# Cross attention: key products for two batches at once, value products for two batches in the other iterations

## What is computed

```python
def _L0_xattn_ref(query, key_value, Wq, bq, Wk, bk, Wv, bv, Wo, bo):
    H, D, scale = 16, 16, 16 ** (-0.5)
    q = (query @ Wq + bq).reshape(B, Nq, H, D).transpose(0, 2, 1, 3)
    k = (key_value @ Wk + bk).reshape(B, Nkv, H, D).transpose(0, 2, 1, 3)   # Nkv = 257, B = 64
    v = (key_value @ Wv + bv).reshape(B, Nkv, H, D).transpose(0, 2, 1, 3)
    attn = jnp.clip(jnp.einsum('bhqd,bhkd->bhqk', q, k) * scale, -CLAMP, CLAMP)
    attn = jax.nn.softmax(attn, axis=-1)
    x = jnp.einsum('bhqk,bhkd->bqhd', attn, v).reshape(B, Nq, Cq)
    return x @ Wo + bo
x = x + _L0_xattn_ref(_layernorm(x), ctx_768, ...)
```

## Time and profile before

| | |
|---|---|
| median of 3 runs | 593.39 us (592.71 to 594.58) |
| the profiled execution | 592.44 us |
| span of its trace, first to last instruction | 590.6 us |
| TensorE busy / weight loads busy | 579.2 us (98%) / 479.8 us (81%) |
| VectorE / ScalarE / POOL busy | 459.9 / 350.9 / 329.3 us |
| first `scores` of the loop | 18.34 us |
| last `scores` (iteration 63) | 328.11 us |
| granted TensorE clock, mean | 0.997 |

### The profile page before, as it was taken

The page is one execution under the profiler, slowest core; times in us unless marked ns, Lnnn a source line. Parts: engine busy times, 40 slices in busy tenths (PEclk is TensorE's granted clock), DMA queues, the critical chain, the costliest instruction groups (busy, mean ns, idle before and its releaser), DMA issues.

```text
span 590.6 us, 21921 instructions
## 1 busy us (share of the span) xinstructions
PE 579.2 (98%) x8431; PEld 479.8 (81%) x8431; DVE 459.9 (78%) x1064; ACT 350.9 (59%) x769; POOL 329.3 (56%) x481
## 2 busy tenths in 40 slices
PE   9999999999999999999999999999899999999997
PEld 4888878888788888788888788888478888887597
DVE  3688867888677887777777687698878888888496
ACT  4677867878777778677776444655433333333363
POOL 3456867878758788578887231011267666663000
PEclk9999999999999999999999999999899999999999
DMA  8625453676545745686430199535634334342895
GB/s 228 190 61 130 139 180 119 202 189 192 177 138 174 199 167 178 199 227 191 150 106 4 22 403 407 208 107 188 250 108 143 133 131 132 134 134 91 290 348 147
DMA packets 65399, 102.13 MB, mean 173 GB/s; under 512 B 15281, under 2 KB 41969, under 8 KB 64401
## 3 DMA queue, kind: packets, MB, share of 16 engines
q1 hardware_dynamic: 59200, 84.40, 45.2%
q0 software_dynamic: 4992, 15.34, 7.8%
q10 hardware_dynamic: 1104, 0.99, 0.6%
HBM read 69.43 MB, written 31.27 MB: 170 GB/s over the span
## 4 chain that ended last, share of the span: by engine, by line
PE 57%; POOL 20%; issue 14%; DVE 6%; DMA 1%; ACT 1%; POOLq 0%; SPq 0%; DVEq 0%
PE bank L2023 12%; PE scores L2023 6%; PE bank L1058 5%; PE bank L1065 5%; PE bank L1090 4%; POOL hA L732 4%; POOL lA L728 4%; PE bank L2051 4%; POOL hA L724 4%; PE scores L1106 3%; PE scores L1079 3%; PE scores L1242 2%; POOL Mb L765 2%; POOL tm L756 2%; PE bank L1017 2%
## 5 line engine op out<-in xcount | busy, mean ns | idle before, releaser
L864 DVE TENSOR_SCALAR Pm<-scores 128x514 f32<-128x514 f32 x128 | 88.1, 689 | 52.2 <-PE scores L1079 52.0
L980 ACT ACTIVATE Pm<-Pm,nm 128x257 f32<-128x257 f32 x256 | 115.7, 505 | 2.5 <-DVE nm L869 2.5
L869 DVE TENSOR_REDUCE nm<-Pm 128x2 f32<-128x514 f32 x128 | 87.5, 684 | 2.2
L975 ACT ACTIVATE PT<-bank 128x512 f32<-128x512 f32 x64 | 38.3, 598 | 74.1 <-PE bank L1090 74.1
L1058 PE MATMUL bank<-hA,wH 128*128 128x258 f32 x256 | 75.2, 305 | 0.1
L1090 PE MATMUL bank<-cst,Pm 128*128 128x128 f32 x512 | 70.0, 279 | 0.0
L1058 PE MATMUL bank<-hA,wL 128*128 128x258 f32 x256 | 69.3, 281 | 0.0
L1065 PE MATMUL bank<-wH,hA 128*128 128x256 f32 x256 | 68.9, 281 | 0.0
L1065 PE MATMUL bank<-wL,hA 128*128 128x256 f32 x256 | 68.8, 280 | 0.0
L2023 PE MATMUL bank<-W,xh 128*128 x208 | 66.6, 401 | 0.6 <-ACT xh L1943 0.6
L765 POOL TENSOR_TENSOR Mb<-Os,rc 128x64 f32<-128x64 f32 x64 | 21.7, 339 | 73.6 <-DVE rc L889 73.2
(11 more groups left out here) (299 smaller groups left out, 1428.7 us busy)
## 6 DMA issues: line engine op xcount, KB each, us to landing
w_d<-whl SPq DMA_DIRECT2D x64, 256.0 KB, 3.2
W<-w_d SPq DMA_DIRECT2D x6, 2048.0 KB, 17.7
wst<-in_W1T SPq DMA_DIRECT2D x32, 256.0 KB, 3.7
cg<-g_d SPq DMA_DIRECT2D x16, 512.0 KB, 5.8
cx<-in_ctxT SPq DMA_DIRECT2D x31, 258.0 KB, 3.0
cx<-in_ctxT SPq DMA_DIRECT2D x62, 129.0 KB, 3.6
bb<-in_b SPq DMA_DIRECT2D x8, 512.0 KB, 6.0
W<-w_d SPq DMA_DIRECT2D x5, 512.0 KB, 5.2
```

What stands on the lines that cost most here:

```text
L864: v.tensor_scalar(Pm[:, i % 2, 2 * p:2 * p + 2, :], S4[:, 2 * p:2 * p + 2, 0:NK], -CLAMP, CLAMP, ALU.max, ALU.min).then_inc(s_cl, 1)
L869: v.tensor_reduce(nm[:, i % 2, 2 * p:2 * p + 2], Pm[:, i % 2, 2 * p:2 * p + 2, :], AX.X, ALU.max, negate=True).then_inc(s_nm, 1)
L975: a.activation(PT[:, i % 2, 0, :, :].rearrange("p a b -> p (a b)"), held("p", i, 0)[:, :], ACT.Copy).then_inc(s_pte[0], 1)
L980: a.activation(Pm[:, i % 2, g, :], Pm[:, i % 2, g, :], ACT.Exp, bias=nm[:, i % 2, g:g + 1]).then_inc(s_ex, 1)
```

## The change

Keys of a pair of batches (2p, 2p+1) now come from one set of 10 products of 512 columns, 256 from each batch. They are made in the even iterations i = 2p-2. The odd iterations make the values of two batches, 20 products of 256 columns. At the edges the loop makes single batches of values: in -1 and 0, and in 61 and 62. The 257th key of all 64 batches is projected once ahead of the loop from `c256`, 4 short products into the bank of `vx`, and copied to `kE` by VectorE with the bias. From there ScalarE writes it for each pair into the last columns of `kT` (`last_keys`). `kT` holds two pairs instead of two batches. The splits on POOL change places: low parts in odd iterations, high parts in even ones, and they run one iteration earlier. `pace` is moved with them, and `wst0` gets another address.

```diff
@@ uses
+        def key_pair(i):
+            if i == -1:
+                return 0
+            return i // 2 + 1 if i % 2 == 0 and i + 2 < T else None
+        def value_batches(i):
+            if i in (-1, 0, T - 2):
+                return (i + 1,)
+            if i == T - 3:
+                return (i + 1,)
+            return (i + 1, i + 2) if i % 2 and i + 2 < T else ()
-        uses = [...] + [(("x",), s_vxe, 2)] + [...]
+        uses = [...] + [(("x",), s_vxe, 4)] + [...]
@@ POOL, loop
-                    j, n = (i + 3) // 2 if i % 2 else (i + 2) // 2, 0 if i % 2 else 2
+                    j, n = ((i + 3) // 2, 2) if i % 2 else ((i + 4) // 2, 0)
@@ VectorE, ahead of the loop
                 qevac(0)
+                for m in range(2):
+                    v.tensor_scalar(kE[:, m, :], held("x")[:, C + T * m:C + T * m + T], bcol[:, 2 + m:3 + m], None, ALU.add
+                                    ).then_inc(s_vxe, 1)
@@ ScalarE
+                def last_keys(p):
+                    if p == 0:
+                        a.wait_ge(s_vxe, 4)
+                    if p >= 2:
+                        a.wait_ge(s_s, 4 * (p - 1))
+                    a.activation(kT[:, p % 2, :, :, NK - 1:NKP],
+                                 kE[:, :, 2 * p:2 * p + 2].unsqueeze(3).broadcast_to([128, 2, 2, 2]), ACT.Copy)
-                    a.activation(kT[:, i % 2, m, :], held("k", i, m)[:, 0:NKP], ACT.Identity, bias=bcol[:, 2 + m:3 + m]
-                                 ).then_inc(s_ke, 1)
+                    a.activation(kT[:, p % 2, m, :, 0:NK - 1],
+                                 held("k", p, m)[:, :].rearrange("p (b n) -> p b n", b=2), ACT.Identity,
+                                 bias=bcol[:, 2 + m:3 + m]).then_inc(s_ke, 1)
@@ TensorE
+                        mm = t.matmul(b[:, :].rearrange("p (b n) -> p b n", b=2), w[:, 128 * m:128 * m + 128],
+                                      c[:, :, 0:NK - 1], start=(e == 0), stop=(e == 4))
...
+                for m in range(2):
+                    for k in range(2):
+                        K = 128 - 64 * k
+                        mm = t.matmul(b[:, C + T * m:C + T * m + T], wA[0:K, k, 128 * m:128 * m + 128], c256[0:K, k, :],
+                                      start=(k == 0), stop=(k == 1), skip_group_check=True)
                 mm.then_inc(s_vx, 1)
                 qproj(0)
...
-                    if i + 1 < T:
-                        for p in range(2):
-                            kproj(i + 1, p)
-                        vproj(i + 1)
+                    if i == 0:
+                        vproj(1)
+                    if key_pair(i) is not None:
+                        for m in range(2):
+                            kproj(key_pair(i), m)
+                    if i != 0:
+                        for b in value_batches(i):
+                            vproj(b)
```

More of the change, by code:

```diff
@@ L217, in build @@
         nm = put("nm", [128, 2, 4])
-        wst.append(put("wst1", [128, 1024]))
+        wst = [put(f"wst{i}", [128, 1024]) for i in range(2)]
         whl.append(put("whl1", [128, 2, 1024], F32R))
@@ L223, in build @@
         pO = S4[:, 3, 272:272 + 4 * VH]
[L225 removed]
+        def key_pair(i):
[8 more added lines that the diff above has]
+            return (i + 1, i + 2) if i % 2 and i + 2 < T else ()
+        uses = [(("t", 0, k), s_t0e, k + 1) for k in range(2)] + [(("x",), s_vxe, 4)] + [(("q", 0, m), s_qe, m + 1) for m in range(2)]
         for i in range(-1, T + 1):
@@ L628, in pace @@
                         sp.wait_ge(s_t, 2 * i)
[L629 to L632, removed]
+                    if n % 4 >= 2:
+                        if i % 2 == 0:
+                            sp.wait_ge(s_k, 2 * key_pair(i) + n % 4 - 1)
+                        else:
+                            sp.wait_ge(s_v, i + n % 4)
                 def load_piece(q, h):
@@ L787, in _ @@
                     if go:
-                        if n == 2:
+                        if n == 2 and i >= 2:
                             g.wait_ge(s_m, i - 1)
@@ L988, in _ @@
                         exps(i, 1)
-                    if i + 1 < T:
-                        kevac(i + 1, 0)
-                        kevac(i + 1, 1)
+                    if i == 0:
+                        vevac(1)
+                    if key_pair(i) is not None:
+                        last_keys(key_pair(i))
+                        kevac(key_pair(i), 0)
+                        kevac(key_pair(i), 1)
                     if 0 <= i < T:
@@ L1052, in terms, with kproj @@
                             (hi1, wH[:, 1, :]), (hi1, wL[:, 1, :])]
[L1054 to L1057, removed]
-                        mm = t.matmul(b[:, 0:NKP], w[:, 128 * m:128 * m + 128], c, start=(e == 0), stop=(e == 4))
+                def kproj(p, m):
+                    b = take("k", p, m)
+                    t.wait_ge(s_lo, 2 * (p + 1))
+                    for e, (c, w) in enumerate(terms(p % 2, slice(0, 2))):
+                        mm = t.matmul(b[:, :].rearrange("p (b n) -> p b n", b=2), w[:, 128 * m:128 * m + 128],
+                                      c[:, :, 0:NK - 1], start=(e == 0), stop=(e == 4))
                     mm.then_inc(s_k, 1)
```

26 lines of the change are left out of this document (12 added, 14 removed).

## The result

The changed kernel takes 595.53 us (median of 12 executions, 593.42 to 600.21), the kernel before 593.56 on the same chip (12 executions, 592.37 to 596.82): ratio 1.0039, 95% interval 1.0021 to 1.0056. It is 0.39% **slower**, where 0.3% faster was forecast; that lies just above the upper end of the range, 595.5. The profiled execution took 596.0 us, its span 594.2 us, 3.6 more than before's 590.6.

A forecast was written before the change was run, and what follows sets the result against it. TensorE was taken to set the loop's pace, until VectorE's 3.61 us round binds. -3.6 + 2.16 - 2.18 + 0.9 + 0.2 + 0 + 0.4 = -2.1 us gave a forecast median of 591.3 us, range 589.5 to 595.5.

The forecast's parts named there:

- Step 1: TensorE's key products in the loop: ten of 512 columns replace twenty, 0.12 us less per pair of iterations, -3.6 us.
- Step 2: Key work moved into iterations -1 and 0 costs +2.16 us; iterations 61 and 62 give back -2.18, VectorE binding.
- Step 3: Ahead of the loop: four short products (8 records) cost +0.9 us, the wait for the copies to `kE` +0.2.
- Step 4: ScalarE in the loop: exponentials behind the second key half still come in time, cost 0, slack only 0.15 us.
- rival A: Exponentials come late and stop TensorE in all 30 odd iterations: 595.8 us, slower; chance 0.2.
- Step 5: POOL in the loop: its late one-off work makes scores or keys wait four or five times, +0.4 us (-0.3 to +1.2).
- its own sign: The POOL step is wrong if keys or scores wait in iterations other than 32, 53 and 56.
- Rival B: Key products of 512 columns start 0.240 us apart because the operand has a break: no pair gain, 595.1 us; chance 0.08.
- Rival D: A product's fixed part hides elsewhere, so a pair saves only 0.04 us: 593.7 us, no change; chance 0.05.
- Rival C: Cheap ends: short products 0.4 us, no wait for `kE`, POOL's waits as before: -3.2 us, 590.2 us; chance 0.22.

The follow-up runs named there:

- after_split: The changed kernel with each 512-column key product made as two of 256 columns, one per batch: 611.11 us, ratio 1.0127, in a longer session (before: 603.69 us).
- after_tail: The changed kernel with `total` moved up in VectorE's order, right behind clip(i, 1), in iterations 61 to 63: 593.38 us, ratio 1.0001.
- after_best: The changed kernel with `total` early at the end, POOL's one-off work moved, a filler product dropped, `kE` copies and a split step earlier: 592.60 us, ratio 0.9984.
- after_again: The changed kernel without an edit, run again in a session where every kernel is some 10 us longer: 606.88 us, ratio 1.0054.
- after_contig: The changed kernel with the key products' moving operand as one run of 512 columns instead of two of 256: 596.61 us, one execution.

## Why the prediction was wrong, by its steps

- **Step 1, the width: right mechanism, mis-sized.** The forecast spacing was 0.228, the measured one 0.231, under the bound of 0.240. Ten products so cost 0.03 more. The first step (210.97 to 211.29) and the way back to scores (213.14 to 213.47) are 0.09 and 0.10 above a step, where before they were 0.08 and 0.09: 0.02 more. And before's average pair takes 9.37, not twice the 4.70 of the earlier trace rows. A pair gains 0.06 in all (0.07 against `after_split`, which undoes the width alone), and 30 pairs give -1.8 instead of -3.6: this is the largest single miss. The gain was the difference of two long sums, 2.40 and 2.28, and 0.003 us in the spacing took a quarter of it. Why the spacing is 0.231 here and 0.228 in the earlier trace rows stays open.
- **Step 2, the work moved forward.** +2.16 was right (S(0) to S(2) has +1.14 of it). The way back failed: the step took VectorE's round as the only bound, 3.61, and missed that `scores(i)` waits for `total(i - 3)`, which VectorE makes late in its round. That gave 4.22, -1.0 instead of -2.18. `after_tail` took the wait away and got 3.50.
- **Step 3, ahead of the loop: mis-sized.** The short products take 1.45, not 0.9 (0.4 to 1.1 was the range): their nearest row was taken to be the transposes' 0.106, and a record of 64 columns costs 0.18. The step also gives 256 columns 0.21 us "at the spacing of step 1", which is 0.12; its bounds of 0.053 and 0.13 a record hang on that, and 0.18 lies above both. The wait for `kE` was right, 0.24 for 0.2.
- **Step 4, ScalarE, and rival A: held.** TensorE never waits for `exps` in the loop. The last copy of keys starts at 213.58, 0.11 behind S (213.47), as computed; the exponentials begin 0.58 later, where 0.49 was computed:

```profile
213.58 0.69 ACT L984 ACTIVATE kT<-bank,bcol 128x512 f32<-128x512 f32 x1 [0.47 <-PE bank L1089]
214.16 0.90 ACT L1007 ACTIVATE Pm<-Pm,nm 128x257 f32<-128x257 f32 x2
```

  They end at 215.06, S + 1.59, where S + 1.51 was computed and S + 1.71 needed. With the 0.05 that the forecast gave to the semaphore that leaves 0.07 us of its slack of 0.15: the chain held, by half of what was computed.
- **Step 5, POOL: right size, incomplete places.** The waits are 0.58, 0.45 and 0.59 in iterations 32, 52 and 56 and 0.28 in 26, 1.9 us in all, against about 1.4 in before's 11, 31, 41, 53 and 55: +0.5 for +0.4. Three of the places are the forecast's own: the keys of 32 and 56, and the scores of 53, whose wait makes iteration 52 long. Iteration 26 it did not name, so by its own sign the step is wrong there. `after_best` puts POOL's last step of the split earlier in iteration 25, and 26 takes 4.63.
- **The sum, mended.** Forecast stretches replaced by these: +3.0 (ahead of the loop: S(0) moved 1.1 by the wide keys, 1.45, 0.24, 0.06 of a later start, and about 0.15 since the first steps of the two key halves are 0.63 and 0.34 us long) + 1.1 - 1.7 + 0.5 - 1.0 = **+1.9 us**. The -1.7 is 29 pairs; the last term holds the tail and the thirtieth. The median is 2.0 longer, with an interval of 1.2 to 3.3. Against the forecast's -2.1 the width makes 1.8 of the difference, the tail 1.2, the stretch ahead of the loop 0.8 and POOL 0.1. In the session of `after_again` the change costs 3.2 us, of which 1.3 is open. The rest of the 3.6 between the two profiled executions is one gap of 0.86 behind the loop and 0.6 in the last stages, where nothing of the change lies.
- **Rival B fell** (no spacing of 0.240, `after_contig`). **Rival D** had a pair gain 0.04 by the rule of the Trainium skill ("TensorE: Matmul & The Clock Gate", section "Back-to-back issue gap"), and forecast 593.7. The pair gains 0.06, nearer to D's 0.04 than to the forecast's 0.12, but the rule's spacing of 0.216 for 512 columns is not seen: 0.231. **Rival C** fell with the 1.45.

The range ended at 595.5, since its upper side was rival A, which needs a chain that held; that steps 1, 2 and 3 could all be off to the same side was not priced. The steps that failed are these three: the gain of the width, mis-sized; the tail, where the wait for `total` was missing; and the short products, mis-sized.

## What to carry to other kernels

Before an iteration is called bound by an engine, list every semaphore that the shortened engine's next step waits for, and where in the other engine's round it is given: here an operation late in a 3.5 us round kept TensorE back for 0.65 us until it was moved up. A product of few columns is not priced by its columns: eight records of 64 columns cost 1.45 us in a start without gaps, where they are paid in full. And where a gain is the small difference of two long rows of products, 0.003 us in the spacing is a quarter of it: its range has to say so.

## What the runs showed of the hardware

- Products in float32 of 64 columns with a new weight each: 0.181 us a record (1.45 / 8), in two kernels; the transposes, with 128 columns and a new weight each, take 0.106, so the columns are not what is paid.
- 512 columns, float32r, with a weight load each: 0.230 or 0.231 us a step, whether the moving operand is one run or two of 256.
- Gaps in TensorE's instruction stream, 0.15 to 1.97 us long, up to four in a loop of 64 iterations: all 29 in 13 traces lie whole multiples of 256 instructions apart (to one record) and end 1.24 to 1.65 us after a packet of 16 KB of instructions.
- The same kernel before took 593.4 to 593.6 us in three sessions and 603.7 in another, with most of the extra behind the loop; the ratios of the changed kernel are 1.0039 (beside 593.56) and 1.0054 (beside 603.69). Why a session is longer stays open.
